# A table of fills, scatters and gathers moved by a step in a two-layer attention and mixture-of-experts kernel

## What is computed

```python
x = x + _L0_xcond_ref(_layernorm(x), ctx, ctx, tau, delta, Wq, bq, Wk, bk, Wv, bv, Wo, bo)
x = x + _L0_ffn_ref(_layernorm(x), router_w, e_bias, Wg, Wu, Wd, SWg, SWu, SWd)
x = x + _L1_xcond_ref(_layernorm(x), ctx, ctx, tau, delta, ...)
x = x + _L1_ffn_ref(_layernorm(x), Wg, W1, W2, W3)
# attention:
scores = jnp.einsum('blhe,bshe->bhls', qh, kh) * tau[:, None, None, :] + delta[:, None, None, :]
a = jax.nn.softmax(scale * scores, axis=-1)
out = jnp.einsum('bhls,bshd->blhd', a, vh).reshape(B, L, D) @ Wo.T + bo
# experts: y = sum over the chosen experts of w * (silu(x Wg) * (x Wu)) Wd
# L0: 8 of 64 chosen within 4 of 8 groups, + a shared feed-forward; L1: 2 of 8
```

## Time and profile before

| What | Value |
|---|---|
| median of three runs | 1405.54 us |
| lowest and highest | 1402.01, 1406.44 us |
| the profiled execution | 1418.99 us |
| its span, first to last instruction | 1417.3 us |
| mean granted TensorE clock | 0.928 of full speed |
| PE busy | 1272.4 us (90%) |
| DVE busy | 827.8 us (58%) |
| POOL busy | 557.1 us (39%) |
| ACT busy | 492.7 us (35%) |

### The profile page before, as it was taken

One profiled execution on the slowest core, in us unless ns is written; L12 is line 12 of the kernel. 1 busy time (PEld: TensorE's weight loads), 2 busy tenths in 40 slices (PEclk: granted clock), 3 DMA queues, 4 the chain that ended last, 5 costly groups with the idle time before them and its releaser, 6 DMA issues. The chain is left out here.

```text
span 1417.3 us, 40365 instructions
## 1 busy us (share of the span) xinstructions
PE 1272.4 (90%) x12838; PEld 980.2 (69%) x12839; DVE 827.8 (58%) x2642; ACT 492.7 (35%) x1255; POOL 557.1 (39%) x706
## 2 busy tenths in 40 slices
PE   5999898999966999999848999999999989999996
PEld 3666565666643788888635666666666779999995
DVE  3467766666746666666445666776676354444442
ACT  1454444344421243344214444444344212212221
POOL 2135555454444101100355655666552223332322
PEclk9999999898977999999967988999899699999998
DMA  4334444335532667875322332333321512533423
GB/s 113 105 110 133 124 131 123 121 115 171 157 118 67 210 201 228 249 221 159 109 76 63 86 87 72 95 90 91 82 68 44 189 40 39 156 93 100 127 66 78
DMA packets 115804, 166.65 MB, mean 118 GB/s; under 512 B 26480, under 2 KB 96768, under 8 KB 114672
## 3 DMA queue, kind: packets, MB, share of 16 engines
q0 software_dynamic: 22672, 58.41, 16.2%
q1 hardware_dynamic: 46496, 54.35, 13.2%
q10 hardware_dynamic: 46560, 52.98, 11.6%
HBM read 87.82 MB, written 63.49 MB: 107 GB/s over the span
## 5 line engine op out<-in xcount | busy, mean ns | idle before, releaser
L1047 DVE TENSOR_REDUCE mx<-banks 112x2 f32<-112x750 f32 x256 | 235.7, 936 | 137.0 <-PE banks L627 111.5
L1894 POOL DMA_INDIRECT xs_d<-xns,idx x160 | 155.1, 969 | 176.6 <-PE banks L651 130.6
L1567 ACT ACTIVATE shared_buf<-banks 125x672 f32<-125x672 f32 x256 | 173.0, 727 | 104.1 <-PE banks L651 94.5
L651 PE MATMUL banks<-attn_buf 18*125 18x112 f32 x3072 | 135.2, 301 | 43.9 <-DVE mx L1047 32.2
L1908 POOL DMA_INDIRECT kept<-y_d,yidx x128 | 123.6, 965 | 119.8 <-issue 91.0
L651 PEld LDWEIGHTS banks<-attn_buf 18*125 18x125 f32 x3072 | 109.8, 198 | 74.3 <-DVE mx L1047 36.7
L919 PEld LDWEIGHTS banks<-xT,attn_buf 128*128 128x128 f32 x1364 | 157.1, 192 | 5.1 <-DVE xT L1433 3.6
L919 PE MATMUL banks<-xT,attn_buf 128*128 128x128 f32 x1364 | 157.4, 275 | 3.3 <-DVE xT L1433 3.3
L864 PE MATMUL banks<-xT,staged 128*128 128x128 f32 x1064 | 142.8, 277 | 6.8 <-DVE staged L1444 6.5
L864 PEld LDWEIGHTS banks<-xT,staged 128*128 128x128 f32 x1064 | 129.1, 192 | 11.5 <-DVE xT L1433 8.1
L627 PE MATMUL banks<-attn_buf 17*112 17x375 f32 x1024 | 123.4, 553 | 7.6 <-ACT shared_buf L1567 7.3
(11 more groups left out here) (214 smaller groups left out, 1957.2 us busy)
## 6 DMA issues: line engine op xcount, KB each, us to landing
shared_buf<-xs_d SPq DMA_DIRECT2D x136, 128.0 KB, 2.5
y_d<-shared_buf ACTq DMA_DIRECT2D x132, 128.0 KB, 2.6
ringbuf<-in_we SPq DMA_DIRECT2D x6, 2176.0 KB, 8.2
ringbuf<-in_we POOLq DMA_DIRECT2D x32, 384.0 KB, 4.7
attn_buf<-attn_buf SPq DMA_DIRECT2D x128, 93.8 KB
attn_buf<-in_ctxT ACTq DMA_DIRECT2D x29, 375.0 KB
xs_d<-zrow ACTq DMA_DIRECT2D x16, 512.0 KB
y_d<-zrow ACTq DMA_DIRECT2D x16, 512.0 KB
```

The costliest lines, as they stand in the source:

```text
L651: last = pe.matmul(bank[SCORES_T[j]][0:KT, t * Q:(t + 1) * Q], kT4[rows, u, i, t * KT:(t + 1) * KT], qT4[rows, u, i, :], start=True, stop= ...
L1047: dve.tensor_reduce(mx[:, i % 2, 2 * p:2 * p + 2], banks[0:Q, 2 * p:2 * p + 2, 0:S], AX.X, ALU.max).then_inc(s_max, 1)
L1567: act.activation(pT[:, slot:slot + 2, :], banks[0:KT, first_bank:first_bank + 2, 0:ST * Q], ACT.Exp, scale=0.25).then_inc(s_exp, 1)
L1894: pool.indirect_dma_start(xs_d[L.number], bass.IndirectOffsetOnAxis(ap=idx[:, b % 2, k:k + 1], axis=0), rows, None).then_inc(s_scat[b % 2] ...
```

## The change

Four edits, each in one place.

1. In the opening of the first attention the fills are 8 instead of 10, they no longer wait for `free[1]` (which stands for DVE's addition of the output bias, L1191, having read `M1`), and they write to the first bank of the transposed scores instead.
2. In `body0` one scatter moves from step 0 to step 1: one at step 0, three at step 1. This touches the 13 bodies from 3 to 15.
3. In `body1` the single gather at step 0 moves to step 1: four there, none at step 0. This touches the 12 bodies from 0 to 11.
4. The 32 gathers ahead of the second attention are cut into pieces. `reached(signal, count)` waits before a piece for a step of another engine: for the shared feed-forward's up projections on PE (`s_sgu`), its down projections (`s_sdn`), the first transposes and query projections (`mm["XT"]`, `mm["Q"]`), and the first score rows (`s_rows`).

```diff
-... ("BO", 0), ("ROW1", 0), ("MAX", 0), ("FILL", 10)),
+... ("BO", 0), ("ROW1", 0), ("MAX", 0), ("FILL", 8)),
...
                         elif j == "FILL":
-                            for sm, v in free[1]:
-                                wait(pe, sm, v)
-                            idle(r, M1)
+                            idle(r, bank[SCORES_T[0]])
...
                         pool.wait_ge(s_zero0, 16)
-                        gather(0, 0)
-                        gather(1, 1, 0, 4)
-                        deviation(0, base)
-                        gather(1, 1, 4, 4)
-                        output_row_numbers(2, 0)
-                        gather(2, 0, 0, 4)
-                        deviation(0, base + 1)
-                        gather(2, 0, 4, 4)
-                        output_row_numbers(3, 1)
-                        gather(3, 1)
-                        normalise(0, base + 2, 2)
+                        opening_gathers()
...
+                def reached(signal, count):
+
+                    pool.wait_ge(signal, count)
+                    hold(pool)
+
+                def opening_gathers():
+
+                    gather(0, 0, 0, 4)
+                    reached(s_sgu, 5)
+                    gather(0, 0, 4, 2)
+                    reached(s_sgu, 6)
+                    gather(0, 0, 6, 2)
+                    reached(s_sgu, 7)
+                    gather(1, 1, 0, 4)
+                    deviation(0, base)
+                    reached(s_sdn, 3 * 4)
+                    gather(1, 1, 4, 2)
+                    reached(s_sgu, 8)
+                    gather(1, 1, 6, 2)
+                    reached(mm["XT"], base + 1)
+                    output_row_numbers(2, 0)
+                    gather(2, 0, 0, 2)
+                    reached(mm["Q"], base + 1)
+                    gather(2, 0, 2, 2)
+                    deviation(0, base + 1)
+                    reached(s_sdn, 4 * 4)
+                    gather(2, 0, 4, 2)
+                    reached(s_rows, base * NQ + 1)
+                    gather(2, 0, 6, 2)
+                    reached(mm["XT"], base + 2)
+                    output_row_numbers(3, 1)
+                    gather(3, 1, 0, 2)
+                    reached(s_rows, base * NQ + 2)
+                    gather(3, 1, 2, 6)
+                    normalise(0, base + 2, 2)
...
                 def body0(n, b):
                     after_scores(n, 0)
                     if in_layer(b, -3):
-                        scatter(L, n - 3, b - 3, 2, 2)
+                        scatter(L, n - 3, b - 3, 2, 1)
                     after_scores(n, 1)
                     if in_layer(b, -3):
-                        scatter(L, n - 3, b - 3, 4, 2)
+                        scatter(L, n - 3, b - 3, 3, 3)
...
                 def body1(n, b):
...
                     if in_layer(b, 4):
                         output_row_numbers(b + 4, b % 2)
-                        gather(b + 4, b % 2, 0, 1)
                     after_scores(n, 1)
                     if in_layer(b, 4):
-                        gather(b + 4, b % 2, 1, 3)
+                        gather(b + 4, b % 2, 0, 4)
```

More of the change, by code:

```diff
@@ L318, in build @@
         SP_ATTN, SP_TAB, SP_LATE, SP_PACK, SP_ROWS, SP_LAST, SP_OPEN = (0, 39), (18, 57), 19, 20, 21, (25, 30, 36), 37
-        FIRST_JOBS = ((("K0", 0), ("V2", 0), ("K1", 0), ("XT", 0), ("Q", 0), ("XT", 1), ("V01", 0), ("K0", 1), ("K1", 1), ("ROW0", 0), ("Q", 1), ("BO", 0), ("ROW1", 0), ("MAX", 0), ("FILL", 10)),
+        FIRST_JOBS = ((("K0", 0), ("V2", 0), ("K1", 0), ("XT", 0), ("Q", 0), ("XT", 1), ("V01", 0), ("K0", 1), ("K1", 1), ("ROW0", 0), ("Q", 1), ("BO", 0), ("ROW1", 0), ("MAX", 0), ("FILL", 8)),
                       (("UP3", 0), ("XT", 0), ("Q", 0), ("DOWN3", 0), ("ROW0", 0), ("XT", 1), ("Q", 1), ("ROW1", 0), ("MAX", 0), ("BO", 0)))
```

## The result

The change made the kernel slower: 1423.80 us against 1409.24, medians of 20 runs each, a ratio of 1.009 (95% interval 1.0063 to 1.0118), where 1385.3 was forecast. The profiled execution of the changed kernel took 1428.44 us (span 1426.8, clock 0.913), 9.45 us more than that of before.

A forecast was written before the change was run, and what follows sets the result against it. PE was taken to set the end everywhere, so other engines' order counts only where PE waits. −3.5 − 9.4 − 4.3 + 0 + 0 − 3.0 = −20.2 us, from 1405.54 to a 1385.3 us median; range 1374 to 1406.

The forecast's parts named there:

- The fills: First attention's opening: fills start earlier, so the first transposed scores start at 35.6 instead of 39.16; −3.5 us.
- One scatter less at step 0: First attention's eight looped bodies: the scatter ends earlier, so DVE's 1.17 us wait before the row maximum goes; −9.4 us.
- One scatter more at step 1: First attention, step 1: the third scatter lies wholly in idle time of POOL and DVE; 0 us.
- the rival: Slower case: step-0 hold stays, three scatters hold DVE at step 1, 0.64 us in 13 bodies; +11.7 us, chance 0.10.
- The clock: First attention's eight looped bodies: half of the 8.65 us over full-clock length comes back with PE's idle time; −4.3 us.
- The gather of the bodies: Second attention's bodies, step 1: the moved gather's 1.24 us fits POOL's idle time before the layer norm; 0 us.
- The cover: Second attention, step 1: POOL's 2.83 us of idle time before veps, taken to hold the moved gather's 1.24 us.
- My ends of −2 and +2: Bounds in us on the body gather's 0, from 12 bodies by 0.17 us.
- The 32 gathers: Ahead of the second attention: gathers in pieces stream through PE's idle stretches; a third of 9.1 us taken, −3.0 us.

The follow-up runs named there:

- e9: Kernel before the change plus ten idle PE records ahead of the first attention's second-group transposed scores, bodies 1 to 15; with the pause 1408.58 us, ratio 0.9943.
- e10: Kernel before the change with only the first attention's scatters moved, to 1, 2, 3, 2 over the steps; with the pause 1404.33 us, ratio 0.9920.
- e11: Kernel before the change with only edit 2, the scatter moved from step 0 to step 1; with the pause 1416.25 us, ratio 1.0015.
- e8: Changed kernel with the second attention's layer norm ahead of the fourth gather at step 1; with the pause 1431.71 us, ratio 1.0062 to the kernel before.
- e18: Kernel before the change plus new fills, opening gathers in pieces, and scatters 1, 2, 3, 2; body gathers as before; with the pause 1398.95 us, ratio 0.9907.
- e13: Kernel before the change plus new fills, opening gathers in pieces, and scatters 1, 2, 3, 2; body gathers as before; without the pause 1310.82 us, ratio 0.9990.

## Why the prediction was wrong

*The fills: right.* −3.5 was forecast, −4.3 read; they end at 32.1 at full clock, and the DMA of the maxima is last.

*One scatter less at step 0: right in size.* 4.70 us instead of 5.96 for that step, 1.26 against the 1.17 taken, in the bodies at full clock. The reason given, a start bound to the scatter's end, held on this chip; that it is DVE alone did not. By the Trainium skill, "SBUF — State Buffer", section "SBUF: two separate sides", GpSimd's lock on the shared port pair holds only a vector operation in a two-port mode or with two inputs in SBUF, and a row maximum out of PSUM is neither. The trace agrees in this: in body 18 PE and ACT stood still in such a pause too, so it isn't that lock.

*One scatter more at step 1: the step that failed in the first attention.* It was taken at nothing, as the reduce of the earlier trace rows starts 0.32 us behind the third scatter's end. The price of the rival, 0.64, is what came: step 1 took 7.19 us instead of 6.54 at full clock. The rival wanted the step-0 stall to stay; both happened, one going, one coming, and at full clock that leaves −0.6 us a body. The gap at the end of step 1 stands in six of the eight bodies.

*The clock: wrong in sign.* −4.3 was forecast. At full clock the eight bodies would have been 8 × (23.13 − 1.26 + 0.65) = 180.2 us, and they were 201.99: 21.8 us went to the clock, 13.2 more than the 8.65 before. I took the clock's loss to shrink with PE's idle time. PE's idle pieces over 0.5 us between 95 and 400 us did shrink, from 22.2 to 12.2 us, and the loss grew; part of that shrinking is itself the half clock, which keeps PE busy where it would have waited. The new gap at the end of step 1 has a stretch at half clock begin 0.2 to 1.6 us into step 2 in six of the eight bodies, mostly of 3.4 us; two of the three stretches of 10.2 us begin at step 0, behind a gap of 1.14 us at the end of step 3 that was 0.6 before. That PE's idle time is the cause e9 shows. Which gaps count, by their length, their place or their distance from each other, no run isolates: before, gaps of 1.3 us eight times cost less clock than the change's of 0.85 and 1.14.

*The gather of the bodies: the term that decided, costed at 0 and measured at 7.0 and 8.4 us without the pause and 11 to 20 with it.* The cover was read from one row, the 2.83 us of the earlier trace rows; that body ran at half clock for a while, which stretches the idle time of GpSimd. In bodies 17 and 18 of the same trace, at full clock, that row has 0.69 us, less than the 1.24 of one gather, and in step 1 of bodies 22 to 25, at full clock too, the norm begins at once behind the third gather, without any cover. In body 22:

```profile
904.53 0.26 POOL L1854 TENSOR_SCALAR veps<-mv 112x1 f32<-112x1 f32 x1
```

And the moved gather took its wait and hold along, 0.57 us. My ends of −2 and +2 rested on nothing nearer.

*The 32 gathers: right in what moves, wrong in what stays.* ACT's stall shrank by 6.8 us, the nearer scores came 5.3 us earlier, and the second body started 0.0 us earlier. By the Trainium skill, "Runtime: NRT & Kernel Launch", section "Instruction fetch mechanics", a taken branch to a page that isn't loaded has to fetch it before execution goes on, and the stall would stay whatever the gathers do. The trace differs in half: 6.84 of 12.89 us went with them, so at least that half isn't the fetch alone.

Sum over the profiled pair: 4.3 of gain at the opening, 8.3 of loss in the eight bodies, 18.5 in the second attention, 12.9 gained elsewhere (3.8 of it in the other bodies), together +9.5, the difference of the two spans. What of the 12.9 is the change's and what is where the half clock fell by chance is not shown.

## What to carry to other kernels

Price a moved instruction by the smallest idle time that its new place has over all bodies, at full clock, and count the waits that travel with it. Where the clock of the engine that sets the time falls after it idles, the sum of its gaps does not tell the loss: two orders whose bodies are equally long at full clock, e10 and e11, took 181 and 205 us for eight of them. Filling one gap with idle matmuls gained 0.57% here. Try the neighbouring place too: the same scatter one step further turned no gain into 0.8%. And look at what a burst ends beside: e8 took the late norm away and put the pause into the next body.

## What the runs showed of the hardware that I had not expected

On some chips PE, DVE and ACT pause behind some bursts of two or more indirect DMAs of GpSimd. In the cases shown it lasted 0.4 to 0.8 us, to 0.8 to 1.0 us after the last one's end, and it broke into the middle of a row of matmuls; behind a single scatter of the first attention's step 0 in the changed kernel there was none. On other chips kernels with the same bursts have no such pause. Bodies of the first attention with the same instructions take 21.2 us there and 23.1 at full clock here, and the kernel 1312 against 1409 to 1424 us. So an order tuned on the one kind is not tuned on the other: e18 gains 0.93% with the pause, e13, the same program, 0.1% without. What on a chip makes the pause, and why it stands behind some bursts and not behind others, no run here tells.
